# Cross-attention, two feed-forwards and a second attention on one core: the first attention's heads go by four and no longer by two

## What is computed

```
x = x + xattn(_layernorm(x), ctx, Wq, Wk, Wv, Wo, bo)        # 16 heads of 64
x = x + ffn(_layernorm(x), ...)                              # shared + 2 experts, hidden 1024
x = x + attention(_layernorm(x), ctx, ctx, mask)             # one head of 256
x = x + int8_linear(_layernorm(x), ...)                      # quantised by the maximum of |x|
```

```
q = patch_embed @ Wq;  k = pixel_embed @ Wk;  v = pixel_embed @ Wv
sim = jnp.einsum('bihd,bjhd->bhij', q, k) * SCALE
attn = jax.nn.softmax(sim, axis=-1)
out = jnp.einsum('bhij,bjhd->bihd', attn, v)
return out.reshape(b, n, h * dh) @ Wo + bo
```

## Time and profile before

| | us |
|---|---|
| median of 3 timed runs | 1028.74 (1027.96 to 1029.76) |
| profiled execution, device time | 1028.21 |
| its span, first to last instruction | 1026.4 |
| TensorE busy | 979.3 |
| VectorE busy | 614.2 |
| ScalarE busy | 502.1 |
| POOL busy | 233.4 |
| half 2 (b = 1, c = 0), from its Q unit to the next Q unit | 20.79 |

### The profile page before, as it was taken

How to read it: one execution, slowest core, us unless ns; L and a number is a source line. 1 busy time by engine, 2 the same in 40 slices (tenths; PEclk the granted TensorE clock), 3 DMA queues, 4 the chain that set the end, 5 groups by cost and what they waited for, 6 DMA issues and landing times.

```text
span 1026.4 us, 20038 instructions
## 1 busy us (share of the span) xinstructions
PE 979.3 (95%) x6876; PEld 827.7 (81%) x6876; DVE 614.2 (60%) x1606; ACT 502.1 (49%) x1198; POOL 233.4 (23%) x296
## 2 busy tenths in 40 slices
PE   5999999999999999999999999989999999999764
PEld 4878888888888888888888888868988888898733
DVE  6865456555565555645655556569665565664567
ACT  4665555555555555555555555544324324234233
POOL 0323333332332333333333333220000000000204
PEclk9999999999999999999999999999999999999985
DMA  9200000000000000000000000003401201202102
GB/s 296 83 2 17 0 15 15 0 15 0 15 15 0 15 15 0 15 0 15 15 0 15 7 8 0 2 32 142 119 2 42 79 0 45 74 1 73 48 1 72
DMA packets 20077, 33.63 MB, mean 33 GB/s; under 512 B 1616, under 2 KB 16496, under 8 KB 19040
## 3 DMA queue, kind: packets, MB, share of 16 engines
q1 hardware_dynamic: 20048, 33.25, 10.6%
HBM read 31.41 MB, written 1.84 MB: 32 GB/s over the span
## 4 chain that ended last, share of the span: by engine, by line
PE 91%; DVE 5%; ACT 2%; issue 1%; DMA 0%; POOL 0%; DVEq 0%; ACTq 0%
PE bank L1222 27%; PE bank L1374 11%; PE bank L1440 11%; PE bank L1263 9%; PE bank L1236 8%; PE bank L1243 8%; PE bank L1204 6%; PE bank L1284 4%; PE bank L1403 2%; PE bank L1423 2%; ACT probs L546 1%; PE bank L1192 1%; PE bank L1411 1%; PE bank L1387 1%; DMA x_all<-in_x 0%
## 5 line engine op out<-in xcount | busy, mean ns | idle before, releaser
L458 POOL TENSOR_TENSOR probs<-probs,row_rcp 112x375 f32<-112x375 f32 x256 | 202.6, 813 | 456.0 <-DVE row_rcp L791 456.0
L786 DVE TENSOR_REDUCE neg_max<-bank 112x1 f32<-112x375 f32 x256 | 128.3, 543 | 125.0 <-PE bank L1236 125.0
L546 ACT ACTIVATE probs<-bank,neg_max 112x375 f32<-112x375 f32 x256 | 144.7, 571 | 95.0 <-DVE neg_max L786 95.0
L647 ACT ACTIVATE hid<-bank,b_col 128x448 f32<-128x448 f32 x96 | 61.0, 635 | 160.4 <-PE bank L1440 158.1
L1263 PE MATMUL bank<-probs_t,v 125*64 125x112 f32 x1536 | 101.9, 267 | 3.6 <-DVE probs_t L796 2.8
L1243 PE MATMUL bank<-ident,probs 112*125 112x112 f32 x768 | 104.0, 271 | 0.0
L1263 PEld LDWEIGHTS bank<-probs_t,v 125*64 125x64 f32 x1536 | 74.6, 136 | 36.4 <-issue 32.0
L1243 PEld LDWEIGHTS bank<-ident,probs 112*125 112x125 f32 x768 | 98.8, 188 | 4.0 <-issue 0.4
L1236 PE MATMUL bank<-k_parts,q_parts 64*112 64x376 f32 x768 | 98.0, 360 | 2.2 <-ACT probs L546 2.2
L1222 PE MATMUL bank<-ctx_hi,wk_hi 128*128 128x376 f32 x256 | 97.5, 381 | 0.8 <-DVE q_parts L776 0.6
L1008 DVE CAST hid_hi<-hid 128x448 fp32r<-128x448 f32 x96 | 37.7, 393 | 100.2 <-ACT hid L647 99.3
(11 more groups left out here) (150 smaller groups left out, 1984.9 us busy)
## 6 DMA issues: line engine op xcount, KB each, us to landing
ctx_raw<-in_ctx_t SPq DMA_DIRECT2D x16, 375.0 KB, 3.4
stage<-in_ffn_up SPq DMA_DIRECT2D x3, 1024.0 KB, 4.8
stage<-in_ffn_down SPq DMA_DIRECT2D x3, 1024.0 KB, 6.8
stage<-in_ctx_t SPq DMA_DIRECT2D x8, 375.0 KB, 4.9
stage<-in_ctx_n SPq DMA_DIRECT2D x8, 375.0 KB
ring_more<-in_ctx_t SPq DMA_DIRECT2D x8, 375.0 KB, 6.5
ring_more<-in_ctx_n SPq DMA_DIRECT2D x8, 375.0 KB
x_all<-in_x SPq DMA_DIRECT2D x1, 1344.0 KB, 14.6
```

Of the source, the lines that this page charges most:

```text
L458: eng.tensor_tensor(probs[r][:, :], probs[r][:, :], row_rcp[:, r:r + 1].broadcast_to([S, C]), ALU.mult).then_inc(probs_ready, 1)
L546: eng.activation(probs[r][:, :], bank[2 + r % 2][0:S, 0:C], ACT.Exp, bias=neg_max[:, r:r + 1], accum_out=row_sum[:, r:r + 1]).then_inc(exp ...
L786: eng.tensor_reduce(neg_max[:, r:r + 1], bank[2 + r % 2][0:S, 0:C], AX.X, ALU.max, negate=True) \
```

## The change

Heads go by four. A half has two **visits** `v`, and a visit's TensorE program is: the scores of four heads in banks 2 to 5 (`quad_scores`), V products of the four heads two visits back in bank 6 (`mix_quad`), and then four times the transposes of one head of the visit before (`turn_probs`) and one unit. All transposes of a half with units go to one bank, 7; in the last half, which has no units, they alternate between 7 and 0. The projection by Wo goes behind the visit's last unit and writes bank 0, the token transposes follow and write bank 1, both banks being the units' between whiles.

Every head of a half has its own `probs`, and four `probs_t` take the transposes: VectorE copies those of heads 0 and 1 of the four, ScalarE those of heads 2 and 3. VectorE takes four maxima at the start of a visit, and the small operations of the layer norm are placed anew. ScalarE empties the first unit of a visit between the third and the fourth exponential. In batch 0 the long weight splits move to the end of the visits.

Of ScalarE's and VectorE's loops the diff shows the new lines alone.

```diff
-            probs = [sb(f"probs{i}", [S, C], F32, attn) for i in range(4)]
-            probs_t = [sb(f"probs_t{i}", [CJ, JT, S], F32, attn) for i in range(2)]
+            probs = [sb(f"probs{i}", [S, C], F32, attn) for i in range(HH)]
+            probs_t = [sb(f"probs_t{i}", [CJ, JT, S], F32, attn) for i in range(QUAD)]
...
+        SCORE_BANKS, HEADS_BANK, TURN_BANK, SUM_BANK, TOKENS_BANK = bank[2:6], bank[6], bank[7], bank[0], bank[1]
+
+        def turn_bank(i, project):
+
+            return TURN_BANK if project or i % 2 == 0 else bank[0]
...
+                    for v in range(2):
+                        visit = 2 * u + v
+                        turning = not (first and c == 0 and v == 0)
+                        if project and c == 1 and v == 0:
                             eng.wait_ge(proj_ready[1], unit_count(u, 7))
                             round_ctx(b + 1)
+                        exponential(visit, v, 0)
+                        exponential(visit, v, 1)
+                        exponential(visit, v, 2)
+                        if project:
+                            unit(u + 1, QUAD * v, 1 - c)
+                        exponential(visit, v, 3)
+                        if project:
+                            unit(u + 1, QUAD * v + 1, 1 - c)
+                        if turning:
+                            probs_out(visit - 1, 2, project)
+                        if v == 1 and not (first and c == 0):
+                            heads_out(u - 1)
+                        if project:
+                            unit(u + 1, QUAD * v + 2, 1 - c)
+                        if turning:
+                            probs_out(visit - 1, 3, project)
+                        if first and v == 1:
                             piece_hi(FFN_PIECE + c)
+                        if project:
+                            unit(u + 1, QUAD * v + 3, 1 - c)
...
                 for c, u, project, bf in halves(b, last):
+                    for v in range(2):
+                        visit = 2 * u + v
+                        turning = not (first and c == 0 and v == 0)
+                        if c == 1 and v == 0 and not first:
+                            eng.wait_ge(x_added, 2 * b)
+                        largest_scores(visit, v, 0)
+                        if c == 1 and v == 0 and not first:
+                            norm_stats(norm2, 0, b - 1)
+                        if project and c == 1 and v == 0:
                             ctx_rest(b + 1)
+                        largest_scores(visit, v, 2)
+                        if turning:
+                            probs_out(visit - 1, 0, project)
+                        if c == 1 and v == 0 and not first:
+                            eng.wait_ge(norm2.step, (2 + NORM_OPS) * (b - 1) + 1)
+                        pair_rcp(visit, v, 0)
+                        if turning:
+                            probs_out(visit - 1, 1, project)
+                        if project:
+                            unit_lo(u + 1, QUAD * v, 1 - c)
+                        pair_rcp(visit, v, 2)
+                        if first:
+                            norm1_steps(8 * c + 4 * v)
+                            norm1_steps(8 * c + 4 * v + 1)
+                        elif c == 1:
+                            if v == 0:
+                                norm_moments(norm2, 0)
+                            norm2_steps(b - 1, 7 * v, 7 * v + 4)
+                        if project and v == 0:
+                            unit_lo(u + 1, 1, 1 - c)
+                        if v == 1 and not first:
+                            heads_rest(u - 1)
+                        if c == 0 and v == 0 and not last:
                             normalise(0, norm1, b + 1, b + 1, xn[0])
+                        if project and v == 0:
+                            unit_lo(u + 1, 2, 1 - c)
...
+                        if first and v == 1:
                             piece_lo(FFN_PIECE + c)
+                        if project and v == 0:
+                            unit_lo(u + 1, 3, 1 - c)
+                        if first and c == 1 and v == 1:
                             eng.wait_ge(wo_rounded, 1)
                             eng.tensor_tensor(wo_lo[:, :, :], wo_sb[:, :, :], wo_hi[:, :, :].bitcast(F32),
                                               ALU.subtract).then_inc(wo_split, 1)
...
+                        if v == 1 and not (first and c == 0):
+                            eng.wait_ge(bo_added, b if c == 0 else b + 1)
+                            x_update(b - 1 if c == 0 else b, u - 1, SUM_BANK)
...
-            def pair_scores(g, u, c, s):
-
-                if s == 0:
-                    eng.wait_ge(proj_used[0], unit_count(u, Q_UNIT))
-                eng.wait_ge(proj_used[(K_UNIT + s // 2) % 2], unit_count(u, K_UNIT + s // 2))
-                if positive(g):
-                    eng.wait_ge(exp_ready, g)
+            def quad_scores(visit, u, c, v):
+
+                for k in (K_UNIT + 2 * v, K_UNIT + 2 * v + 1):
+                    eng.wait_ge(proj_used[k % 2], unit_count(u, k))
+                if positive(visit):
+                    eng.wait_ge(exp_ready, QUAD * visit)
                 heads = [slice(DH * e, DH * e + DH) for e in range(2)]
-                for i, (a, b) in enumerate(split_products(((0, 1), (0, 1)))):
-                    for e in range(2):
-                        m = eng.matmul(bank[2 + e][0:S, 0:CP], q_parts[c][heads[e], a, s // 2, :],
-                                       k_parts[c][heads[e], b, s // 2, :], start=(i == 0), stop=(i == 2))
-                m.then_inc(scores_ready, 2)
-
-            def turn_probs(g, r):
-                eng.wait_ge(probs_ready, g + 1)
+                for p in range(2):
+                    for i, (a, b) in enumerate(split_products(((0, 1), (0, 1)))):
+                        for e in range(2):
+                            m = eng.matmul(SCORE_BANKS[2 * p + e][0:S, 0:CP], q_parts[c][heads[e], a, 2 * v + p, :],
+                                           k_parts[c][heads[e], b, 2 * v + p, :], start=(i == 0), stop=(i == 2))
+                    m.then_inc(scores_ready, 2)
+
+            def turn_probs(visit, v, i, project):
+                eng.wait_ge(probs_ready, QUAD * visit + i + 1)
+                if i == 1 and project:
+                    eng.wait_ge(probs_t_ready[0], 2 * visit + 1)
+                if i == 2:
+                    eng.wait_ge(probs_t_ready[0], 2 * visit + (2 if project else 1))
+                if i == 3 and project:
+                    eng.wait_ge(probs_t_ready[1], 2 * visit + 1)
+                if i == 3 and not project:
+                    eng.wait_ge(probs_t_ready[0], 2 * visit + 2)
                 for j in range(JT):
-                    t = eng.transpose(bank[4 + r % 2][0:CJ, j * S:(j + 1) * S], probs[r][:, j * CJ:(j + 1) * CJ],
-                                      ident[0:S, 0:S])
+                    t = eng.transpose(turn_bank(i, project)[0:CJ, j * S:(j + 1) * S],
+                                      probs[QUAD * v + i][:, j * CJ:(j + 1) * CJ], ident[0:S, 0:S])
                 t.then_inc(turned_ready, 1)
...
+            def mix_quad(u, c, v):
+
+                if v == 0:
...
                 for e in range(2):
-                    eng.wait_ge(probs_t_ready[e], HH // 2 * u + s // 2 + 1)
-                for j in range(JT):
-                    for e in range(2):
-                        m = eng.matmul(heads_bank[c][DH * e:DH * e + DH, (s // 2) * S:(s // 2 + 1) * S],
-                                       v_sb[c][:, j, (s + e) * DH:(s + e + 1) * DH], probs_t[e][:, j, :],
-                                       start=(j == 0), stop=(j == JT - 1))
-                m.then_inc(heads_ready, 2)
+                    eng.wait_ge(probs_t_ready[e], 2 * (2 * u + v) + 2)
+                for p in range(2):
+                    for j in range(JT):
+                        for e in range(2):
+                            s = QUAD * v + 2 * p + e
+                            m = eng.matmul(HEADS_BANK[DH * e:DH * e + DH, (s // 2) * S:(s // 2 + 1) * S],
+                                           v_sb[c][:, j, s * DH:(s + 1) * DH], probs_t[2 * p + e][:, j, :],
+                                           start=(j == 0), stop=(j == JT - 1))
+                    m.then_inc(heads_ready, 2)
...
                 for c, u, project, bf in halves(b, last):
-                    for s in range(0, HH, 2):
-                        g, n = HH * u + s, HH * c + s
-                        pair_scores(g, u, c, s)
+                    for v in range(2):
+                        visit = 2 * u + v
+                        turning = not (first and c == 0 and v == 0)
+                        quad_scores(visit, u, c, v)
+                        if not (first and c == 0):
+                            mix_quad(u - 1, 1 - c, v)
+                        if last and c == 1 and v == 0:
                             eng.wait_ge(gate_step, 4)
```

(54 more changed lines are left out.)

206 lines of the change are left out of this document (72 added, 134 removed).

## The result

The kernel after takes 1011.97 us in the median of four runs (1010.56 to 1014.48), the kernel before beside it 1029.24 us (1027.96 to 1029.76); the ratio is 0.9837, 95% interval 0.9815 to 0.9859. It is faster by 1.6%, as forecast, and lies inside the forecast's range, but 7 us above the forecast time of 1005. The profiled execution took 1010.56 us with a span of 1008.8, where that of before took 1028.2 with 1026.4. So the two traces have 17.6 us between them to explain, where 22.9 were forecast.

A forecast was written before the change was run, and what follows sets the result against it. TensorE's own stream was taken to bound the kernel, busy 95% of the span. 30.9 us saved in thirty halves, less 3.0, 1.5, 2.1 and 1.4, gave 22.9 off 1028.2: 1005 us, forecast 996 to 1012, wider range 996 to 1018.

The forecast's parts named there:

- the switch of shape: Scores and V products: two round trips a half instead of four, blocks 5.02 us instead of 5.68, saving 0.66.
- The seam inside the doubled blocks: Second pair inside a block pays no switch; at worst 0.09 + 0.05 per block pair, 0.28 us a half.
- Neighbours: Steps beside the blocks, per half: 0.18 and 0.44 us saved, 0.08 and 0.20 lost to transposes.
- Q's bank: Unit 2 waits for VectorE's subtraction to free Q's bank: no slack, 0.1 us a half, 3.0 in all.
- Bank 1 with norm2's small operations: Second half of a batch: norm work delays unit 1's subtraction, unit 3 due then; 0.1 us in 15 halves, 1.5.
- Batch 0: Long weight copies at visit ends delay x_update and the next Q unit: cost 2.1 us (0 to 4).
- The last half: One chain through the engines without units, split_shared ahead of the next four maxima: cost 1.4 us (-1 to 3).
- (a): Rival: handovers in each visit lose 0.3 to 0.6 us a half more, giving 1014 to 1023 us; chance 0.20.
- (b): Rival: VectorE's and ScalarE's copies set the pace, slower than before, 1061 us; chance 0.08.
- (c): Rival: gain and waits cancel, 0.9 to 1.1 us lost a half, 1028 to 1034; chance 0.07 with (d).
- (d): Rival: extra step belongs to each accumulation group, not shape changes; 1029 to 1032 us; chance 0.07 with (c).
- (e): Rival: no waits at all and no loss in batch 0, 995 to 997 us; chance 0.05.

The follow-up runs named there:

- the late copy: Kernel after with one more VectorE operation of about 0.65 us per half, directly ahead of the subtraction that frees Q's bank: 1028.3 us.
- short products: Kernel after with GpSimd multiplying only the first 75 of 375 columns of each head's probabilities, the rest left unscaled: 1008.6 us.
- the first experiment: Kernel after with scores and V products done pair by pair again, four round trips a half instead of two: 1030.4 us in one run.
- the last kernel: Kernel after with batch 0 and the last half rearranged and the first half of piece_lo(5) moved behind visit 3's second reciprocal: 998.84 us, ratio 0.9706 to before.

## Why the prediction was right, and where it was not

- **What bounds the kernel, and the switch of shape.** Right, to the hundredth where it counts: 1.20 and 1.30 us for the blocks against 1.21 and 1.30; 0.68 us a half by the return to four round trips, against 0.66; for all 0.99 against 1.03. The seam inside the doubled blocks costs nothing that can be seen, as taken: 1.20 and 1.30 leave no room for its 0.09 and 0.05.
- **Neighbours.** +0.18 + 0.44 - 0.08 - 0.20, which is 0.34, rounded up to 0.37: measured 0.99 - 0.68 = 0.31, as a remainder; no run takes its parts to pieces.
- **Turned heads in one bank:** cost 0, right. No wait for probs_t between 100 and 600 us.
- **Q's bank:** the mechanism (no slack) was right, by the late copy and by the matmul that starts 0.06 us behind the subtraction. The size was off: 3.0 us charged, nothing paid that the trace shows. The forecast's "due 3.39, released 3.41" gives 0.02 a half, and the 0.1 was caution on top; in the trace unit 2 starts 3.41 us after Q (488.26 to 491.67), in even steps. The forecast's own figures do not quite add up either: a copy that ends at 2.8 and a subtraction of 0.63 end at 3.43, and not at 3.36.
- **Bank 1 with norm2's small operations:** 1.5 us charged, 0 paid. In the middle halves norm2's slow operations fall where nobody waits: both kinds of half are 19.80 us.
- **Batch 0: the step that failed.** Charged 2.1 us (0 to 4), paid 4.7 + 2 x 0.99 = 6.7 us. The one wait that it named came as forecast (3.6 us for x_all against 3.1 + 0.4). Four things were missing or too small in the term. The copy of unit 7 behind the rounding of ffn_up cost 1.6 us, not 1.0. The subtraction that frees unit 1's bank stood behind norm1's operations, and two of these took 0.74 and 0.73 us beside GpSimd's products, 0.24 with short ones (a wait of 1.5 us, 0.5 with short products). The first copy of turned heads at 34.4 us stood behind the norm's statistics and four maxima (1.2 us). And the long wait was followed by the clock at half, 1.65 us more in the stretch behind it. Laying batch 0 out anew brings the whole of it back (81.9 to 74.4 us), which is 0.7 us better than before's 77.1 less 2 x 0.99.
- **The last half: the second step that failed.** Charged 1.4 us (-1 to 3), paid 4.0 + 0.99 = 5.0. The place was named (split_shared ahead of the next four maxima), the size not: with norm2's operations the maxima start at 653.56 us, 3 us after their scores, and Wo's matmuls then run at half clock (0.21 us a step instead of 0.12). Left out was a second wait, 2.2 us ahead of Wo's product, which needs heads_lo: this stood behind three of norm2's operations of 0.73 us each beside a GpSimd product (656.90 to 659.09). What GpSimd adds is a large part of the 5.0: with short products and the same order the stretch is 2.7 us shorter, clock included, though the products' own link of the chain is shorter there too. Another order of the same work brings back 3.6 us.
- **Feed-forward and tail:** 0 charged, 0.3 paid.

By stretch: the middle was 2.9 us better than its forecast (26.6 against 27 x 0.88 = 23.8), the start 4.4 worse, the last half 3.5 worse, the rest 0.3; that is the 5.3 us between 1005.3 and the 1010.6 of the profiled execution. Of the rivals, (a) began at 1014, which is nearly the time, but for a reason that the runs exclude: the handovers of the middle lost nothing. (b) is excluded for this kernel by the 19.80 us, though only just: VectorE's copy of Q has no slack, and 0.59 us more on it cost 0.60. The Trainium skill's warning in TensorEngine Tiling (Array Packing), "PSUM Bottleneck", that the copy out of PSUM may become the bound, holds here at the edge, for one of eight units. (c) and (d) are excluded by the halves and by the first experiment. (e), 995 to 997 us, is nearly reached once both ends are put in order: 998.8 us. That the forecast came out only 5.3 us low is in part luck: a middle better by 2.9 us covered a third of what the two ends lost beyond their terms.

What stays open is which idle stretches bring the clock down. It fell after waits of 3.6, 3.5, 2.8 and 1.8 us, after one of 1.6 us in a single profile out of seven that have it, and in the last half of two kernels whose longest waits there were 1.4 and 1.2 us; in the last kernel it did not fall, with waits of up to 1.2. No run here isolates that.

## What to carry to other kernels

When many equal steps in the middle of a kernel get shorter, cost its first and last rounds by themselves, instruction by instruction: they carry the work that occurs once, and here they gave back 11.7 of the 29.7 us that the steady part gained. Keep operations of over 1 us that nobody waits for out of the queue ahead of a short one that TensorE needs, and cut them in two where the idle times are short; if a wait goes away, look who else stood behind the same operation. Mark which of VectorE's operations would run beside one of GpSimd's, and cost them at the length that they have there. A wait list that is empty does not prove slack: delay the suspected producer and see whether the period moves.

## What the runs showed of the hardware

- **VectorE waits for a whole GpSimd product.** The timeline of the kernel after, where norm2's small operations meet two products (start, length, engine, operation):

```profile
183.06 1.58 POOL L460 TENSOR_TENSOR probs<-probs,row_rcp 112x375 f32<-112x375 f32 x2 [0.23 <-DVE row_rcp L807]
```

```profile
183.08 0.82 DVE L756 TENSOR_TENSOR norm_term<-norm_term,norm_half 112x1 f32<-112x1 f32 x1
183.93 0.74 DVE L758 SCALAR_TENSOR_TENSOR norm_bits<-norm_term,norm_bits 112x1 f32<-112x1 f32 x1
```

  An operation on one element a row, begun 0.02 us behind a product, ends 0.02 us behind that product (0.81 us long), and the next one behind the second. Between 30 and 665 us all 32 cases of L756 and L758 that overlap a product take 0.73 to 0.82 us, and all 64 that overlap none take 0.14 to 0.17. Both read two tensors. L746 and L748 read one: 31 of theirs overlap a product and all are fast (0.14 to 0.17). The Trainium skill has this rule, which the forecast did not use: SBUF — State Buffer, "Who interferes with whom", says that a VectorE instruction with two SBUF inputs, or in a two-port mode, and a GpSimd instruction that reads SBUF exclude each other, and that the one which starts second waits for the whole of the other. The trace agrees for operations with two inputs. Some with one input are slower beside a product too: split_shared's cast (0.61 to 0.98 us), and the normalisation of 112x256 (L773), which takes 0.90 us in the 13 cases between 100 and 600 us that begin beside a product and 0.41 in the 13 others; in which mode they run no trace here shows. In the kernel before three of 208 small operations (30 to 685 us) took over 0.5 us, because its products fell elsewhere. The three that norm2 repeats (135 of them) take 25.7 us there (45 to 690 us) and 41.5 in the kernel after (45 to 670 us), and the normalisations 6.9 us more than before. These 22.7 us are more than VectorE's 16.5 (the maxima, for one, take 4.9 less). With short products VectorE's busy time is 606.6 us, and not 630.7.
- **The clock after a wait.** TensorE was at half clock for 3.5 to 10.5 us (read in windows of 0.5 us) behind waits of 1.8, 2.8, 3.5 and 3.6 us, at places where the kernel before ran at 1.00. It made a wait of 3.6 us cost 5.3.
- **A change of the array's shape** cost 0.34 us for each extra round trip from scores to V products inside a visit (0.68 us for two).
